# Full expert blocks by table and one last block per expert, a preparing step ahead of the blocks, and gathers taken one by one between the feature operations

## The chip, the cores and the metric

One core of a Trainium2 chip runs the whole program. The metric is the device time of one execution in microseconds (us), median of several runs. TensorE, VectorE, ScalarE, GpSimd and SyncE (here only an issuer of DMAs) each run their own stream of instructions and meet at semaphores. In the rows PE is TensorE's matmul, PEld its weight load, DVE VectorE, ACT ScalarE, POOL GpSimd, SPq the sequencer of SyncE.

## The reference

Input x has 32 batches of 256 tokens of 128 elements. With xn = layernorm(x) the result is x + attention(xn) + ffn(xn):

```python
# attention: 16 heads of 8, per batch, over 256 tokens
cov = einsum('bhsd,bhtd->bhst', q - mean(q), k - mean(k)) / 8
scores = cov + var(q)[..., :, None] * var(k)[..., None, :] / 8
out = softmax(scores) @ v @ Wo
# ffn: causal attention across the 32 batches for each token place, then experts
x1 = x + causal_attention(layernorm(x))
hn2 = layernorm(x1)
topw, topi = top_k(softmax(hn2 @ router_w.T), 2)        # 2 of 8 experts
y = sum over the two: gate * (gelu(hn2 @ w1[e]) @ w2[e])  # 128 -> 256 -> 128
return x1 + y
```

## The kernel before

The program has three stages, and every engine's stream is written out in their order.

**Groups** (`group_step`, g = -3 to 16, 16 groups of 16 token places by 32 batches = 512 rows each): the causal attention, x1, the router. The two chosen experts' rows of a token, `rows`, are scattered by GpSimd's indirect DMAs into the HBM tensor `token_rows` at places `spots`; each expert has a region of its own there. `scatter(n, p, k)` issues four of them, for k = 0 and 1. `add_x` adds x to x1 into `acc`, which SyncE stores as `out_base`. Step 16 is the last of the stage, with only the router part of group 15; GpSimd's step 15 ends with `add_x(15)`, then `scatter(14, .., 1)`, `scale_x(1)` and `scatter(15, .., 0)`.

**Blocks** (`blocks`, 40 blocks of 512 rows): VectorE's `block_table` counts each expert's rows and makes a table of 40 starts and owners. With C rows an expert has as many blocks as 512 goes into C, rounded up; its last start is clamped so that the block ends with the expert's rows, and so it overlaps the block before it, which is why the stores keep an order. SyncE loads rows and weights six blocks ahead (`load_block`), TensorE transposes the rows (`turn`), multiplies up (`expert_up`), ScalarE takes the gelu (`hidden`), TensorE multiplies down (`expert_down`), VectorE multiplies by the gate (`expert_y`, three buffers `y_sb`), and GpSimd stores to `expert_out` (`store_blocks`, line 620), each store after the one before has landed:

```python
pool.wait_ge(s_y, i + 1)
if i >= 1:
    pool.wait_ge(s_yd[(i - 1) % YBUFS], 16 * ((i - 1) // YBUFS + 1))
```

**Steps** (`step(b, p)`, b = -1 to 32, one batch each; `rest_steps`): the attention of xn. A step goes through 16 heads. TensorE makes the column scores of batch b's heads and, four heads ahead, the row scores of batch b + 1 (from head 12 on of b + 2), of which VectorE takes maxima (`take_max`, `rowmin`, line 1182); the maxima become `shift` rows (`split_shift`, lines 1190 and 1192, at heads 3 and 12). ScalarE takes the exponentials. Batch b + 3 is prepared at the same time: VectorE's statistics at head 0, GpSimd's `scale_x` (lines 488, 490, tile `centre`), ScalarE's `normalise_x` at head 5, TensorE's transposes at head 7 and projection at head 9, ScalarE's `features`, then GpSimd's `features_stack`: four operations of squares (lines 500 to 508), the high part (510, 513), the low part (two copies, 516, and two subtracts, 518). TensorE transposes that stack (`stack_transposes`, line 721) in the next step, half 0 at head 9 and, one step on, half 1 at head 0 (`PE_AT`), and VectorE copies it out. GpSimd also gathers the expert rows of batch b by four indirect DMAs (`gather`, line 604, tile `ysel`, which the rows call `xg`) and sums them (`add_selected`, line 610); TensorE adds the sum at head 13 of the next step (`project_out`). `own.next()` is GpSimd's wait for its own last operation.

Each engine has the order: groups, blocks, then steps -1 to 32. Step -1 has no scores of its own: it makes the maxima of batch 0 and the first four of batch 1, and prepares batch 2. TensorE starts the blocks after four maxima, and begins step -1 when y of the last block is done.

## Time and profile before

| | |
|---|---|
| median of 3 runs | 1063.92 us (1061.32 to 1064.46) |
| profiled execution, own time | 1062.73 us |
| its span, first to last instruction | 1060.8 us |
| busy, share of the span | PE 85%, DVE 77%, ACT 66%, POOL 58% |
| mean granted TensorE clock | 0.937 of full speed |
| groups, blocks, steps | to about 366 us; 382 to 540; 540 to the end |

The profile is of one execution. Starts are counted from the first instruction. A busy share says how long instructions of an engine were under way, and matmuls overlap, so a full TensorE need not be at its peak; what sets the time is read from waits, stage by stage.

### The profile page before, as it was taken

The page shows a single profiled execution, that of the slowest core. Times are in us where ns is not written, and L with a number is a line of the kernel's source. Part 1 is how long each engine was busy: PE and PEld are TensorE (multiplying, and loading weights), DVE is VectorE, ACT ScalarE, POOL GpSimd, SP SyncE. Part 2 cuts the span into 40 slices and gives each one's busy share as a digit, 9 for nine tenths or more (in the row PEclk, how much of TensorE's full clock was granted, in tenths as well). Part 3 has the DMA queues.
Part 4 walks back from the last instruction along what each step waited for, and adds up shares of the span by engine and source line. Part 5 has one row for each costly group of instructions (what it writes and reads, how often), then busy time and mean ns, then how long its engine had stood idle before and what let it go on. Part 6 is the DMA issues. An engine that isn't in the chain of part 4 may idle for free.

```text
span 1060.8 us, 34080 instructions
## 1 busy us (share of the span) xinstructions
PE 901.2 (85%) x11947; PEld 563.1 (53%) x11962; DVE 819.3 (77%) x2175; ACT 696.2 (66%) x1395; POOL 613.1 (58%) x886
## 2 busy tenths in 40 slices
PE   3677887878886449999969999999999999999997
PEld 2445554655654237877734555555555555555543
DVE  4876877788787435555558999999999999999980
ACT  3666877788784213433316778777777877777774
POOL 4145666667677531211127777777777777777741
PEclk9688999899999659999977999999999999999998
DMA  5419322223221147777521111111111111111111
GB/s 154 80 31 200 74 53 56 60 53 72 52 50 35 43 132 214 215 219 204 172 61 38 38 48 51 40 42 46 48 34 46 51 33 48 46 46 36 43 42 31
DMA packets 110825, 80.52 MB, mean 76 GB/s; under 512 B 23297, under 2 KB 97921, under 8 KB 110721
## 3 DMA queue, kind: packets, MB, share of 16 engines
q1 hardware_dynamic: 99328, 51.78, 19.5%
q0 software_dynamic: 11392, 27.35, 8.8%
q8 instruction: 66, 1.08, 0.5%
q14 instruction: 39, 0.31, 0.1%
HBM read 44.83 MB, written 33.73 MB: 74 GB/s over the span
## 4 chain that ended last, share of the span: by engine, by line
PE 41%; DVE 18%; issue 16%; DMA 12%; ACT 10%; POOL 2%; DVEq 1%; POOLq 0%; SPq 0%; ACTq 0%
PE bank L682 34%; DMA expert_out<-y 11%; DVE rowmin L1182 7%; PE bank L721 3%; ACT Vexp L1657 2%; DVE QKT L1173 2%; ACT gxb L1685 2%; PE bank L804 1%; ACT rows L1700 1%; DVE smax L1227 1%; ACT hnT L1628 1%; PE bank L783 1%; POOL token_rows L554 1%; DVE sprobT L1238 1%; ACT prob L1664 1%
## 5 line engine op out<-in xcount | busy, mean ns | idle before, releaser
L1613 ACT ACTIVATE prob<-bank 128x512 f32<-128x512 f32 x512 | 293.1, 603 | 88.7 <-PE bank L682 86.2
L1182 DVE TENSOR_REDUCE rowmin<-bank 128x2 f32<-128x512 f32 x512 | 325.6, 683 | 32.0 <-PE bank L682 29.6
L682 PE MATMUL bank<-QKT 32*128 32x256 f16 x2048 | 184.7, 276 | 28.4 <-DVE rowmin L1182 21.9
L604 POOL DMA_INDIRECT xg<-expert_out,place x128 | 125.1, 978 | 46.7 <-issue 31.0
L554 POOL DMA_INDIRECT token_rows<-rows,spots x128 | 127.2, 994 | 40.2 <-issue 32.3
L682 PEld LDWEIGHTS bank<-QKT 32*128 32x128 f16 x2048 | 67.0, 93 | 143.4 <-DVE rowmin L1182 68.7
L682 PE MATMUL bank<-prob,V 128*25 128x256 f32 x2048 | 137.8, 387 | 0.5 <-ACT prob L1613 0.5
L1772 ACT ACTIVATE hmid<-bank,wrow,up_scale 128x512 f32<-128x512 f32 x80 | 58.0, 773 | 107.7 <-PE bank L682 107.7
L620 POOL DMA_DIRECT2D expert_out<-y x40 | 30.2, 755 | 134.9 <-DMA expert_out<-y 106.5
L682 PEld LDWEIGHTS bank<-prob,V 128*25 128x25 f32 x2048 | 50.5, 103 | 52.0 <-issue 26.6
L682 PE MATMUL bank<-wrow,hmid 128*128 128x128 f32 x640 | 77.8, 275 | 0.0
L682 PEld LDWEIGHTS bank<-wrow,hmid 128*128 128x128 f32 x640 | 74.6, 192 | 0.1
L1491 DVE TENSOR_TENSOR y<-bank,xrow 128x512 f32<-128x512 f32 x40 | 27.7, 692 | 54.3 <-DMA expert_out<-y 50.6
L1227 DVE TENSOR_REDUCE smax<-bank 128x16 f32<-128x512 f32 x64 | 43.8, 684 | 32.4 <-PE bank L682 29.8
L500 POOL TENSOR_TENSOR sq<-feat 128x512 f32<-128x512 f32 x32 | 33.3, 1040 | 59.0 <-ACT feat L1584 58.9
L682 PE MATMUL bank<-turned,wrow 128*128 128x512 f16 x240 | 61.0, 392 | 7.4 <-DVE turned L1483 7.2
L682 PE MATMUL bank<-hnT,in_wT 128*128 128x512 f32 x64 | 42.6, 752 | 25.0 <-ACT hnT L1628 21.5
L539 POOL TENSOR_TENSOR rstd<-var,minus_half 128x4 f32<-128x4 f32 x16 | 16.6, 1037 | 64.4 <-DVE minus L1274 64.4
L682 PE MATMUL bank<-Kexp,gqT 32*32 32x128 f32 x2048 | 39.6, 308 | 16.5 <-issue 16.4
L1238 DVE STREAM_TRANSPOSE sprobT<-prob 128x512 f32<-128x512 f32 x64 | 43.4, 697 | 9.0 <-ACT prob L1664 8.6
L1481 DVE CAST turned<-bank 128x512 f16<-128x512 f32 x40 | 27.5, 686 | 27.4 <-PE bank L989 27.4
L1644 ACT ACTIVATE Kexp<-bank,head_bias,quad_mask 128x512 f32<-128x512 f32 x64 | 44.4, 775 | 5.5 <-PE bank L682 5.5
(229 smaller groups left out, 1945.9 us busy)
## 6 DMA issues: line engine op xcount, KB each, us to landing
xrow<-token_rows SPq DMA_DIRECT2D x40, 258.0 KB, 3.0
wrow<-weight_rows SPq DMA_DIRECT2D x40, 257.0 KB, 3.2
expert_out<-y POOLq DMA_DIRECT2D x40, 256.0 KB, 2.8
token_rows<-xrow SPq DMA_DIRECT2D x16, 258.0 KB
xg<-in_L_attn_x SPq DMA_DIRECT2D x64, 64.0 KB, 2.2
x_in<-in_L_attn_x SPq DMA_DIRECT2D x32, 128.0 KB
out_base<-acc SPq DMA_DIRECT2D x64, 64.0 KB
base_t<-out_base SPq DMA_DIRECT2D x32, 128.0 KB
```

What stands on the lines that cost most here:

```text
L500: pool.tensor_tensor(sq[:].rearrange(flat), eight, eight, ALU.mult).then_inc(s_pool, 1)
L554: pool.indirect_dma_start(token_rows, bass.IndirectOffsetOnAxis(spots[p][:, j:j + 1], 0), rows[p][:, k, t, :].bitcast(U32), None).then_inc ...
L604: pool.indirect_dma_start(ysel[p][:, k, st, :].bitcast(U32), None, expert_out, bass.IndirectOffsetOnAxis(place[p][:, st, k:k + 1], 0)).the ...
L620: pool.dma_start(expert_out[bass.ds(at, BLK), :].rearrange("(s p) e -> p s e", p=P), y_sb[i % YBUFS][:].bitcast(U32)).then_inc(s_yd[i % YB ...
L682: return pe.matmul(o, l, r, start=start, stop=stop, skip_group_check=True)
L721: ins = pe.transpose(m[:, a, g, st], stack[p][:, a, st, h:h + TILE_ROWS, :].rearrange("p h k -> p (h k)"), identh[:])
L1182: dve.tensor_reduce(rowmin[h // 8][:, :, h % TILE_ROWS, h // TILE_ROWS % HALF], row_scores[i % 3][:].rearrange("p (s t) -> p s t", s=ST), ...
L1227: dve.tensor_reduce(smax[:, r, :], ps, AX.X, ALU.max).then_inc(s_dve, 1)
L1238: dve.transpose(sprobT[:, r].rearrange("p h s -> p (h s)"), sprob[:, r].rearrange("p h s -> p (h s)")).then_inc(s_spT[r], 1)
L1613: act.activation(prob[:, h % 8].rearrange("p t s -> p (t s)"), col_scores[h % 2][:], ACT.Exp, scale=exp_register).then_inc(s_exp, 1)
L1644: ins = act.activation(Kexp[:, :, j, :], head_bank[:].rearrange("p (n t) -> p n t", n=GPOS), ACT.Identity, bias=head_bias[:, j:j + 1], sca ...
L1772: act.activation(hmid[i % 2][c][:], up_bank[c][:], ACT.Gelu, bias=w[:, c:c + 1], scale=up_scale[:, 0:1]).then_inc(s_mid, 1)
```

## The change

1. **Table for the full blocks only.** `FULL` = 32 entries of starts and owners, of blocks filled to the last row (512 goes into C, rounded down). Then every expert has exactly one last block, whose start `tail_at` is max(C - 512, 0) in its region. There are 40 blocks as before. `block_numbers` makes the constant parts ahead of the counts, the running sums are made in three doubling steps instead of seven, and the limits go. The stores of the full blocks wait for no other store; the first last block waits for all full ones, and the last blocks wait for none among them.
2. **Step -1 ahead of the blocks** on GpSimd, TensorE, VectorE and ScalarE, with `shift_out(0, 1)` of step 0 behind it; SyncE keeps it behind its block loads. TensorE's waits ahead of `turn(0)` grow to the end of that step (`s_half[0]` 2, `s_feat` 3, `s_sht[1]` 1, `s_max` 20).
3. **GpSimd's step.** `features_stack` is split in three. `features_low` runs in the next step; `add_selected` does too; the four gathers stand between the pieces. `add_x` of a group moves behind `scatter(g - 1, .., 1)` and `scales(g + 3)`.

GpSimd's order in one step of the steady loop is, before (`DMA` is a gather, `xg` its tile, `sq` and `feat` the features):

```order
L488 TENSOR_TENSOR rstd<-var_x,minus_half 128x2
L490 TENSOR_TENSOR centre<-minus_mean,rstd 128x2
L597 ISA
L600 TENSOR_TENSOR spare<-epsilon 1x1
L604 DMA xg<-expert_out,place 128x128 x4
L500 TENSOR_TENSOR sq<-feat 128x512
L502 TENSOR_TENSOR sq<-sq 128x64x4
L505 TENSOR_TENSOR sq<-sq 128x64x2
L508 TENSOR_TENSOR sq<-sq 128x64
L510 TENSOR_SCALAR feat<-sq,var_scale 128x64
L513 CAST stack<-feat 128x64x9
L516 COPY stack<-stack 128x32x9 x2
```

and now, from the start of a step to its squares:

```order
L489 TENSOR_TENSOR rstd<-var_x,minus_half 128x2
L491 TENSOR_TENSOR centre<-minus_mean,rstd 128x2
L616 ISA
L617 TENSOR_TENSOR xg<-xg 128x256
L604 ISA
L607 TENSOR_TENSOR spare<-epsilon 1x1
L611 DMA xg<-expert_out,place 128x128
L521 COPY stack<-stack 128x32x9 x2
L523 TENSOR_TENSOR stack<-feat,stack 128x32x9 x2
L611 DMA xg<-expert_out,place 128x128
L497 REGISTER_ALU
L501 TENSOR_TENSOR sq<-feat 128x512
```

The sum of the rows (L617) and the low part (L521, L523) are those of the batches before, and stand ahead of the squares of this step; the other two gathers follow the squares and the high part.

TensorE's order ahead of block 0 (`xrow`) was:

```order
L682 MATMUL bank<-wqk,xnT 128x2x128 x2
L682 MATMUL bank<-QKT 128x256 x8
L989 MATMUL bank<-ident,xrow 128x128 x4
L682 MATMUL bank<-turned,wrow 128x512 x6
L989 MATMUL bank<-ident,xrow 128x128 x4
```

and is now, from the transposes of batch 2 in step -1 on:

```order
L724 MATMUL bank<-ident,xn 128x128 x2
L712 MATMUL bank<-QKT 128x256 x4
L751 MATMUL bank<-identh,stack 128x128 x8
L712 MATMUL bank<-wqk,xnT 128x2x128 x2
L712 MATMUL bank<-QKT 128x256 x8
L834 MATMUL bank<-identh,shift 16x128 x2
L712 MATMUL bank<-QKT 128x256 x4
L1019 MATMUL bank<-ident,xrow 128x128 x4
L712 MATMUL bank<-turned,wrow 128x512 x6
```

The row scores (`QKT`), the stack and shift transposes and the projection of step -1 moved from behind the last block to ahead of the first.

The diff, cut (renamed and new small tiles and most of the table are left out):

```diff
@@ -65,7 +65,8 @@
 COLS = TOPK * TILES
 BLK = 512
 SUBS = BLK // P
-BLOCKS = TOPK * NB * NS // BLK + NE
+FULL = TOPK * NB * NS // BLK
+BLOCKS = FULL + NE
 CAP = NB * NS + BLK
 XROWS = NE * (CAP + BLK)
 ROWW = E + 1
...
@@ -489,7 +490,7 @@
                 pool.wait_ge(s_pool, own.next())
                 pool.tensor_tensor(centre[:], minus_mean[:], rstd[:], ALU.mult).then_inc(s_rstd, 1)
 
-            def features_stack(n, p):
+            def features_squares(n):
 
                 pool.wait_ge(s_feat, n + 1)
                 if positive(n - 1):
@@ -507,11 +508,15 @@
                 pool.wait_ge(s_pool, own.next())
                 pool.tensor_tensor(sq[:, :, :, 0], sq[:, :, :, 0], sq[:, :, :, 1], ALU.add).then_inc(s_pool, 1)
                 pool.wait_ge(s_pool, own.next())
...
+
+            def features_high(p):
                 pool.tensor_scalar(feat[:, :, :, D], sq[:, :, :, 0], var_scale[:, 0:1], None,
                                    ALU.mult).then_inc(s_pool, 1)
                 pool.wait_ge(s_pool, own.next())
                 pool.tensor_copy(parts[p][:, :, 0:FEAT], feat[:].rearrange(flat)).then_inc(s_pool, 1)
                 pool.wait_ge(s_pool, own.next())
+
+            def features_low(p):
                 for a in range(2):
                     pool.tensor_copy(slots[p][:, a, :, 1 + a, :], slots[p][:, a, :, 0, :])
...
@@ -575,21 +580,23 @@
                     scale_x(0)
                 if tail:
                     scales2(g)
-                    add_x(g, r)
                 if late:
                     scatter(g - 1, 1 - p, 1)
                 if isinstance(g, int) and g == GROUPS - 2:
-                    features_stack(0, 0)
+                    features_squares(0)
+                    features_high(0)
+                    features_low(0)
                 if isinstance(g, int) and g == GROUPS - 1:
                     scale_x(1)
                 if ahead:
                     scales(g + 3)
                 if tail:
+                    add_x(g, r)
                     scatter(g, p, 0)
                 if isinstance(g, int) and g == -3:
                     clear_values()
...
-            def gather(n, p):
+            def gather_ready(n, p):
 
                 if isinstance(n, int) and n == 0:
                     for k in range(YBUFS):
@@ -599,11 +606,11 @@
                     pool.wait_ge(s_pr_ps, n - 1)
                 pool.tensor_tensor(spare[:], epsilon[0:1, 0:1], epsilon[0:1, 0:1], ALU.add).then_inc(s_pool, 1)
                 pool.wait_ge(s_pool, own.next())
-                for k in range(TOPK):
-                    for st in range(ST):
-                        pool.indirect_dma_start(ysel[p][:, k, st, :].bitcast(U32), None, expert_out,
-                                                bass.IndirectOffsetOnAxis(place[p][:, st, k:k + 1], 0)
-                                                ).then_inc(s_sel[p], 16)
+
+            def gather(p, k, st):
+                pool.indirect_dma_start(ysel[p][:, k, st, :].bitcast(U32), None, expert_out,
+                                        bass.IndirectOffsetOnAxis(place[p][:, st, k:k + 1], 0)
+                                        ).then_inc(s_sel[p], 16)
 
             def add_selected(n, p):
                 pool.wait_ge(s_sel[p], n * 32 + (64 - 32 * p))
...
@@ -613,10 +620,14 @@
 
                 pool.wait_ge(s_table, 1)
                 for i in range(BLOCKS):
-                    at = pool.value_load(table[0:1, 0, i:i + 1], min_val=0, max_val=XROWS - BLK)
+                    if i < FULL:
+                        at = pool.value_load(table[0:1, 0, i:i + 1], min_val=0, max_val=XROWS - BLK)
+                    else:
+                        at = pool.value_load(tail_at[0:1, i - FULL:i - FULL + 1], min_val=0, max_val=XROWS - BLK)
+                    if i == FULL:
+                        for k in range(YBUFS):
+                            pool.wait_ge(s_yd[k], 16 * ((FULL - k + YBUFS - 1) // YBUFS))
                     pool.wait_ge(s_y, i + 1)
-                    if i >= 1:
-                        pool.wait_ge(s_yd[(i - 1) % YBUFS], 16 * ((i - 1) // YBUFS + 1))
                     pool.dma_start(expert_out[bass.ds(at, BLK), :].rearrange("(s p) e -> p s e", p=P),
                                    y_sb[i % YBUFS][:].bitcast(U32)).then_inc(s_yd[i % YBUFS], 16)
 
@@ -624,14 +635,30 @@
                 prev, cur, nxt, prep, norm = present(b)
                 own.count = 0
                 pool.sem_clear(s_pool)
+                first = isinstance(b, int) and b == 0
                 if norm:
                     scale_x(b + 3)
+                if prev:
+                    add_selected(b - 1, 1 - p)
+                if cur and not first:
+                    gather_ready(b, p)
+                    gather(p, 0, 0)
+                if prep and not first:
+                    features_low(p)
+                if cur and not first:
+                    gather(p, 0, 1)
+                if norm:
+                    features_squares(b + 3)
+                if first:
+                    gather_ready(b, p)
+                    gather(p, 0, 0)
+                    gather(p, 0, 1)
                 if cur:
-                    gather(b, p)
+                    gather(p, 1, 0)
                 if norm:
-                    features_stack(b + 3, 1 - p)
+                    features_high(1 - p)
                 if cur:
-                    add_selected(b, p)
+                    gather(p, 1, 1)
 
             def masks():
                 pool.memset(onesb[:], 1.0)
...
@@ -670,7 +697,10 @@
                     pool.wait_ge(s_vones, q + 1)
 
             run_groups(pool, group_step)
-            features_stack(1, 1)
+            features_squares(1)
+            features_high(1)
+            step(-1, 1)
+            features_low(0)
             store_blocks()
             rest_steps(pool, step)
...
@@ -1016,9 +1046,10 @@
 
                 pe.wait_ge(s_spot, GROUPS)
                 pe.wait_ge(s_zeroed, 2)
-                pe.wait_ge(s_half[0], 1)
-                pe.wait_ge(s_feat, 2)
-                pe.wait_ge(s_max, 4)
+                pe.wait_ge(s_half[0], 2)
+                pe.wait_ge(s_feat, 3)
+                pe.wait_ge(s_sht[1], 1)
+                pe.wait_ge(s_max, H + LEAD)
                 turn(0)
                 for i in range(BLOCKS):
                     expert_up(i)
@@ -1101,6 +1132,7 @@
                             pv(b, p, g)
 
             run_groups(pe, group_step)
+            step(-1, 1)
             blocks()
             rest_steps(pe, step)
 
@@ -1352,6 +1384,8 @@
                         bias_columns()
                     for r in range(1, QUAD):
                         block_transposes(g, r)
+                if isinstance(g, int) and g == GROUPS:
+                    block_numbers()
                 if late:
                     choose_values(g - 1)
                     choose_experts(g - 1)
...
-            def block_table():
...
+            def block_numbers():
...
                 dve.memset(number[:, 0:1], 0.0).then_inc(s_dve, 1)
...
-                dve.tensor_scalar(limit_at[:, 0:NE], count[:], -float(BLK), 0.0, ALU.add, ALU.max)
...
+                dve.tensor_scalar(row_end[:], number[:], float(BLK), float(BLK), ALU.mult, ALU.add).then_inc(s_dve, 1)
...
+            def block_table():
...
+                                  row_end[:, 0:most].unsqueeze(1).broadcast_to([1, NE, most]), ALU.is_ge)
+                dve.tensor_scalar(tail_row[:], count[:], -float(BLK), 0.0, ALU.add, ALU.max).then_inc(s_dve, 1)
...
-                for e in range(1, NE):
+                dve.tensor_copy(tail_at[:], tail_row[:])
...
+                for k in range(3):
...
+                    dve.tensor_tensor(ends[k][:, d:NE], last[:, d:NE], last[:, 0:NE - d], ALU.add).then_inc(s_dve, 1)
...
-                    dve.tensor_tensor(ends[:, e:e + 1], ends[:, e - 1:e], filled[:, e:e + 1], ALU.add).then_inc(s_dve, 1)
...
-                dve.tensor_tensor(past[:], number[:].unsqueeze(2).broadcast_to([1, BLOCKS, NE]),
...
-                dve.tensor_tensor(begin[:], begin[:], limit[:], ALU.min).then_inc(s_dve, 1)
...
+                dve.tensor_tensor(past[:], number[:].unsqueeze(2).broadcast_to([1, FULL, NE]),
...
@@ -1548,6 +1580,7 @@
             for i in range(LEAD):
                 take_max(0, i)
             dve.memset(pv_bank[:], 0.0).then_inc(s_zeroed, 1)
+            step(-1, 1)
             blocks()
             rest_steps(dve, step)
 
@@ -1787,7 +1820,7 @@
                         copy_out(b - 1)
                     if h == ACT_AT["features"] and norm:
                         features(b + 3)
-                    if h == ACT_AT["shift1"] and cur:
+                    if h == ACT_AT["shift1"] and cur and not (isinstance(b, int) and b == 0):
                         shift_out(b, 1)
                     if h == ACT_AT["v"] and nxt:
                         v_out(b + 1, 1 - p)
@@ -1803,6 +1836,8 @@
             run_groups(act, group_step)
             act.wait_ge(s_scales, 1)
             act.reg_load(exp_register, exp_scale[0:1, 0:1].bitcast(U32))
+            step(-1, 1)
+            shift_out(0, 1)
             blocks()
             rest_steps(act, step)
 
@@ -1924,11 +1959,16 @@
                 k = i % XBUFS
                 if i >= XBUFS:
                     sp.wait_ge(s_y, i - XBUFS + 1)
-                at = sp.value_load(table[0:1, 0, i:i + 1], min_val=0, max_val=XROWS - BLK)
-                of = sp.value_load(table[0:1, 1, i:i + 1], min_val=0, max_val=(NE - 1) * P)
+                if i < FULL:
+                    at = sp.value_load(table[0:1, 0, i:i + 1], min_val=0, max_val=XROWS - BLK)
+                    of = sp.value_load(table[0:1, 1, i:i + 1], min_val=0, max_val=(NE - 1) * P)
+                    weights = weight_rows[bass.ds(of, P), :]
+                else:
+                    at = sp.value_load(tail_at[0:1, i - FULL:i - FULL + 1], min_val=0, max_val=XROWS - BLK)
+                    weights = weight_rows[(i - FULL) * P:(i - FULL + 1) * P, :]
                 sp.dma_start(xrow[k][:].bitcast(U32), token_rows[bass.ds(at, BLK), :].rearrange("(s p) c -> p s c", p=P)
                              ).then_inc(s_bx[k], 16)
-                sp.dma_start(wrow[k][:].bitcast(U32), weight_rows[bass.ds(of, P), :]).then_inc(s_bx[k], 16)
+                sp.dma_start(wrow[k][:].bitcast(U32), weights).then_inc(s_bx[k], 16)
 
             def clear(at):
 
@@ -1965,7 +2005,7 @@
             for p in range(2):
                 sp.wait_ge(s_accd[p], 64 * GROUPS // 2)
                 sp.wait_ge(s_placed[p], 16 * GROUPS // 2)
-            rest_steps(sp, step)
+            rest_steps(sp, step, -1)
             for p in range(2):
                 sp.wait_ge(s_out[p], 16 * NB // 2)
 
```

## Rows read from the trace of the kernel before

**Rows 1.** The chain that ended last, shares of the span by line.

```profile
PE bank L682 34%; DMA expert_out<-y 11%; DVE rowmin L1182 7%; PE bank L721 3%; ACT Vexp L1657 2%; DVE QKT L1173 2%; ACT gxb L1685 2%; PE bank L804 1%; ACT rows L1700 1%; DVE smax L1227 1%; ACT hnT L1628 1%; PE bank L783 1%; POOL token_rows L554 1%; DVE sprobT L1238 1%; ACT prob L1664 1%
```

**Rows 2.** Windows: us, busy us and (x) instructions by engine, PEclk, DMA share, GB/s.

```profile
395.00:427.00 32.00, 32.00 (x238) 25.73 (x236) 18.86 (x28) 13.01 (x18) 5.41 (x7) 1.00 0.66 193
...
540.00:576.00 36.00, 28.18 (x215) 13.99 (x216) 26.61 (x59) 15.31 (x31) 18.20 (x30) 0.63 0.14 39
656.00:1000.00 344.00, 328.93 (x3906) 180.62 (x3906) 321.98 (x668) 269.74 (x579) 257.72 (x397) 1.00 0.16 44
```

**Rows 3.** Timeline (start us, us, engine, line, operation): VectorE's y; TensorE's last down projection.

```profile
395.15 0.69 DVE L1491 TENSOR_TENSOR y<-bank,xrow 128x512 f32<-128x512 f32 x1 [0.37 <-PE bank L682]
...
426.82 0.69 DVE L1491 TENSOR_TENSOR y<-bank,xrow 128x512 f32<-128x512 f32 x1 [0.37 <-PE bank L682]
...
539.18 0.69 DVE L1491 TENSOR_TENSOR y<-bank,xrow 128x512 f32<-128x512 f32 x1 [2.70 <-DMA expert_out<-y]
...
535.77 0.39 PE L682 MATMUL bank<-wrow,hmid 128*128 128x128 f32 x2
```

**Rows 4.** Timeline of GpSimd in group step 15, and VectorE's last table operations.

```profile
350.60 1.26 POOL L563 TENSOR_TENSOR acc<-x,xg 128x512 f32<-128x512 f32 x1
352.03 1.04 POOL L554 DMA_INDIRECT token_rows<-rows,spots  x1 [0.17 <-issue]
...
372.71 0.17 DVE L1475 CAST table<-owner 1x40 int32<-1x40 f32 x1
```

**Rows 5.** Chain of waits ahead of block 0: start us, us, what.

```profile
374.85 2.27 DMA token_rows<-rows,spots
...
382.31 1.10 PE bank L989 x4
```

**Rows 6.** Timeline of GpSimd, VectorE and TensorE behind the blocks, steps -1 to 1.

```profile
547.38 0.74 POOL L488 TENSOR_TENSOR rstd<-var_x,minus_half 128x2 f32<-128x2 f32 x1
548.20 0.20 POOL L490 TENSOR_TENSOR centre<-minus_mean,rstd 128x2 f32<-128x2 f32 x1
...
556.03 2.47 DVE L1182 TENSOR_REDUCE rowmin<-bank 128x2 f32<-128x512 f32 x4
...
558.00 1.03 PE L721 MATMUL bank<-identh,stack 128*128 128x128 f16 x8
...
575.62 0.62 PE L721 MATMUL bank<-identh,stack 128*128 128x128 f16 x8
```

**Rows 7.** Timeline of GpSimd in a step of the steady loop.

```profile
780.12 1.09 POOL L604 DMA_INDIRECT xg<-expert_out,place  x1 [0.51 <-POOL spare L600]
781.51 0.94 POOL L604 DMA_INDIRECT xg<-expert_out,place  x1 [0.30 <-issue]
...
786.78 1.04 POOL L500 TENSOR_TENSOR sq<-feat 128x512 f32<-128x512 f32 x1 [1.83 <-ACT feat L1584]
...
789.60 0.56 POOL L510 TENSOR_SCALAR feat<-sq,var_scale 128x64 f32<-128x64 f32 x1
...
791.02 0.87 POOL L516 COPY stack<-stack 128x288 f16<-128x288 f16 x2
791.85 1.42 POOL L518 TENSOR_TENSOR stack<-feat,stack 128x288 f16<-128x288 f32 x2
793.22 0.74 POOL L610 TENSOR_TENSOR xg<-xg 128x256 f32<-128x256 f32 x1
...
794.72 0.19 POOL L490 TENSOR_TENSOR centre<-minus_mean,rstd 128x2 f32<-128x2 f32 x1
...
795.59 1.08 POOL L604 DMA_INDIRECT xg<-expert_out,place  x1 [0.51 <-POOL spare L600]
```

**Rows 8.** Timeline of VectorE and TensorE in the same step.

```profile
780.85 0.33 DVE L1190 TENSOR_SCALAR shift<-rowmin 128x16 f16<-128x16 f32 x1
...
787.79 0.18 DVE L1190 TENSOR_SCALAR shift<-rowmin 128x16 f16<-128x16 f32 x1
...
784.53 0.62 PE L721 MATMUL bank<-identh,stack 128*128 128x128 f16 x8
```

85 lines of the change are left out of this document (39 added, 46 removed).

## The prediction

> **What bounds the kernel now.** I read the chain of waits first, then windows by stage, then each engine's timeline at the seams. The chain [rows 1] names matmuls for a third of the span and, second, the stores `expert_out<-y` with 11%: in the expert stage the pacing is done by a DMA. The windows [rows 2] show three regimes: from 395 to 427 us TensorE has no gap and full clock; from 540 to 576, the seam between expert blocks and attention, it is busy 28 of 36 us at a granted clock of 0.63, most of that time on the lower of its two levels (1.2 of 2.4 GHz), after 3 us without work; from 656 to 1000, steady attention, TensorE (329 of 344 us) and VectorE (322) are both almost full and GpSimd has a quarter free.
>
> *Expert stage.* y(0) starts at 395.15 and y(9) at 426.82 [rows 3]: 3.52 us a block, and VectorE waits only 0.37 us for TensorE there. From y(9) to y(39) at 539.18 it is 112.36 us for 30 blocks, 3.75 us each, because each store waits for the one before it. TensorE had done its last down projection at 536.16 (535.77 + 0.39) and y(39) came 3 us later.
>
> *Ahead of the blocks.* The last scatter is issued at 374.85 and lands 2.27 us later; TensorE transposes block 0 at 382.31 [rows 5]. In between the only large work is GpSimd's for batch 1.
>
> *Behind the blocks.* Step -1 needs `centre` of batch 2, which GpSimd makes only after its last store, at 548.40; the last row maximum ends at 558.50; the stack transposes of step 0 (its first head) are at 558.00 and those of step 1 at 575.62, 17.62 us later [rows 6], against 15.47 us in the steady loop (two first gathers, 780.12 and 795.59 [rows 7]). I take 15.5.
>
> **The change, part by part** (the sum is against the profiled execution: span 1060.8, own time 1062.73; the median of the runs, 1063.92, is 1.2 higher).
>
> 1. `add_x` behind the scatter. In steps 0 to 14 the same GpSimd work is only permuted inside one step, and `gb`, which comes 1.3 us earlier, feeds ScalarE work that then waits longer for TensorE: nothing. In step 15 the add (1.26 us) stood ahead of the scatters, and everything up to block 0 hangs on them: they start 0.17 us after `rbias` instead of at 352.03 [rows 4], 1.2 us earlier.
>
> 2. Table. It becomes shorter, but was ready at 372.9 with the scatters landing at 377.1 [rows 4, 5]: nothing now. The maxima behind it start some 3 us sooner and step -1 with them, which the next term needs.
>
> 3. Step -1 ahead of the blocks. TensorE now waits for 20 maxima, so block 0 waits for the whole step. GpSimd sets it: its last scatter is issued from 374.85 on, takes 0.94 (the length of a second gather [rows 7]) and now ends at 374.6; squares and high part of batch 1 take 4.2 (786.78 to 790.95 for the same operations [rows 7]): 378.8; `scale_x(2)` takes 1.0 [rows 6]: 379.85. From `centre` to the last maximum it was 558.50 - 548.40 = 10.1 [rows 6], at the same low clock: block 0 starts at 390.0, 7.7 us later than at 382.31. The low part of batch 1 (2.25, the time of the two copies and two subtracts [rows 7]) ends at 382.1, as TensorE gets there.
>
> 4. Stores without order. y(0) comes 12.84 us after block 0's transposes [rows 3, 5]: 402.8. At 3.52 a block y(38) starts at 536.6. The last block has no transposes and no up projection behind it: y(39) starts about 1.9 later, 538.5, and ends at 539.2, where before it ended at 539.87. So the blocks end 0.7 us earlier although they began 7.7 later. The one wait left, all full stores ahead of the first of the last eight, stands on GpSimd beside a 3.5 us block and costs nothing.
>
> 5. Step 0 right behind the blocks. The stack transposes came 0.6 after y(39) in step -1; now it is step 0 that begins so: 539.8 for 558.00, 18.2 us less. TensorE arrives warm, so step 0 takes 15.5 for 17.6: another 2.1. Together 20.3 us.
>
> 6. GpSimd's new order, the term that takes back. The low part of the features moves into the next step, behind `scale_x`, the sum of the gathered rows and the first gather, and TensorE needs it at head 9. That closes a loop: squares, low part, stack transposes, projection, features, squares. Each piece, from [rows 7]: four square operations 2.7 (786.78 to 0.1 before 789.60); gather 0.51 + 1.09; high part 1.37; gather 1.6 (7.3 so far); `scale_x` 1.0 (8.3); the sum waits for the gather issued at 6.2. The nearest row for its landing is the scatter's 2.27 with an issue of 0.94 [rows 5]; with 1.09 of issue I take 2.4: 8.6. Sum of the rows 0.74, spare 0.2, gather 1.6: 11.1. Low part 2.27: 13.4. From the transposes at 784.53 [rows 8] to the next squares at 786.78: 2.25. The loop is 15.7 us, 0.2 more than the step. Before, the low part was ready at 793.27 and used a step later at head 9, 6.8 us of slack; now there is none. The first round is longer: in step 0 the spare operation and three gathers stand between squares and high part, two of them at 0.30 + 0.94: loop 18.4, 2.9 over the step. So 2.9 + 28 x 0.18 = 7.9 us are lost, TensorE waiting at head 9. Bounds for the loop: 15.4 if a landing takes no longer than `scale_x` and the semaphore gaps are 0.30 as between two gathers, 16.2 if the gather, which reads rows of HBM instead of writing them, lands 0.5 us later. I take 15.7, nearest the rows.
>
> The Trainium skill, in "DMA: Bandwidth & Descriptors", section "Rules for kernel authors", says to issue a DMA early, compute, and wait for it late. That speaks against this edit, which leaves `scale_x` alone between the last gather and its wait, and puts whatever landing remains into the loop. With that page's fixed cost of about 2.0 us for a transfer, as an estimate, the sum would wait about nothing and the loop be some 15.4 us.
>
> Sum: -20.3 + 7.9 = -12.4; 1062.7 becomes 1050.3, and with the 1.2 us between profiled run and median **1051.5**.
>
> **The rivals.**
>
> *A. The loop does not bind.* GpSimd keeps 15.5 or less and only the first round costs 2 us. Moreover the pair `shift` at head 3 now meets a gather in progress (0.33 us, ending with it at 781.2 [rows 7, 8]; the one at 787.79 takes 0.18) and would meet GpSimd between two operations: 0.15 x 29 = 4 us. Time 1063.9 - 20.3 + 2 - 4 = 1041.6 at the best, 1045.6 without that. For it: GpSimd has a quarter free. Against it: the loop's pieces add up past the step. The Trainium skill, in "SBUF — State Buffer", section "Who interferes with whom", has VectorE's two-port modes and GpSimd exclude each other for a whole instruction; by that rule such a gain exists, and the trace agrees with the 0.33. Chance 0.25.
>
> *B. The loop is longer than 16.1.* Slower than before needs (20.3 - 2.9) / 28 = 0.62 us a step over 15.5, that is a landing 0.45 us later than I take, or VectorE holding GpSimd up at each gather. At 16.3: 28 x 0.8 = 22.4, and 1063.9 - 20.3 + 2.9 + 22.4 = 1069. No row shows a gather's landing, which speaks neither way; GpSimd's operations have the same durations in every step shown, which speaks against. Loops of 15.9 to 16.1 (1058 to 1063.5) have 0.08, slower ones 0.09.
>
> *C. The stores gain nothing:* unordered stores run into the loads, and the pace stays 3.75 a block instead of 3.52. For it: the chain has 11% on these stores [rows 1], and the DMA engines are at 0.66 [rows 2]. Against: that share is the one of the stretch that ran at 3.52. It costs 30 x 0.23 = 7: 1058.5. Chance 0.1. That the change doesn't store a row twice or skip one is clear from its table, so "does nothing" has no share of its own.
>
> **How the numbers follow.** Forecast (loop 15.5 to 15.9, pace 3.52): 0.48, 1046 to 1058, likeliest 1051.5. A 0.25, B's two parts 0.17, C 0.1. The range for 8 in 10 reaches from A at its best, 1041, to a loop of 16.05, 1062. A measurement of this kernel tells 0.3%, 3.2 us, from no change: faster is the forecast, A, C and most of the loops below 16.0, 0.84; within 0.3% (1060.7 to 1067.1) 0.09; slower 0.07.
>
> **What would show it.** Right: y(0) near 403 and 3.52 us a block to y(38); stack transposes of step 0 within 1 us of y(39); clock 1.0 through step 0; GpSimd's feature subtract ending just ahead of the transposes at head 9, with TensorE waiting there for it each step; gathers' first to first 15.7. Wrong: block 0 before 388 or after 393; GpSimd waiting over 1 us for `feat` in the steady loop (then A); the row sum over 1 us behind `centre` (then B); VectorE's y waiting for stores (then C).

## The result: 1034.84 us, faster, and below the forecast range

The changed kernel took 1034.84 us (median of 4 runs, 1033.28 to 1042.30), the kernel before 1064.19 on the same chip: a ratio of 0.9731, interval 0.9680 to 0.9783. Forecast were 1051.5 and 1041 to 1062. The direction was right; the gain was 17 us larger than forecast. Some runs of a kernel are over 1.5% above its fastest; the ratios here and below leave those out, and for the first chip of the experiments, where six of the seven runs of the kernel before were such (1267.58 to 1273.43, the seventh 1248.46), no ratio is given. The profile below is of the 1042.30 run, the slowest of the four.

The chain that ended last, by line; against [rows 1] the stores are gone from it and GpSimd's feature and gather work has come in.

```profile
PE bank L712 36%; POOL xg L611 4%; POOL stack L523 3%; DVE rowmin L1214 3%; PE bank L751 2%; POOL stack L521 2%; PE bank L1019 2%; POOL rstd L489 2%; POOL sq L501 2%; ACT Vexp L1690 2%; ACT gxb L1718 2%; ACT rows L1733 1%; DVE sprobT L1270 1%; POOL sq L503 1%; POOL token_rows L559 1%
```

The windows of [rows 2], of the kernel after (columns as there: busy us and instructions of TensorE, its weight loads, VectorE, ScalarE, GpSimd, then granted clock, DMA share, GB/s). The seam (540 to 576) is warmer than before, 0.76 for 0.63, and holds 288 matmul records for 215; the steady stretch does 3998 in the time in which it did 3906.

```profile
395.00:427.00 32.00, 30.39 (x193) 22.78 (x194) 15.25 (x23) 11.80 (x16) 4.68 (x6) 0.85 0.43 132
540.00:576.00 36.00, 30.25 (x288) 15.36 (x288) 25.12 (x55) 20.54 (x43) 18.28 (x27) 0.76 0.12 35
656.00:1000.00 344.00, 334.41 (x3998) 183.84 (x3995) 314.88 (x679) 268.65 (x590) 268.65 (x407) 1.00 0.17 45
```

Timeline around the blocks, answering [rows 3, 5, 6]: block 0's transposes, y of block 0, of block 9 and of the last, then the stack transposes of steps 0 and 1.

```profile
392.50 1.09 PE L1019 MATMUL bank<-ident,xrow 128*128 128x128 f32 x4 [1.60 <-DVE rowmin L1214]
...
406.03 0.69 DVE L1523 TENSOR_TENSOR y<-bank,xrow 128x512 f32<-128x512 f32 x1 [0.78 <-PE bank L712]
437.70 0.69 DVE L1523 TENSOR_TENSOR y<-bank,xrow 128x512 f32<-128x512 f32 x1 [0.37 <-PE bank L712]
541.08 0.69 DVE L1523 TENSOR_TENSOR y<-bank,xrow 128x512 f32<-128x512 f32 x1 [1.10 <-PE bank L712]
...
542.15 0.62 PE L751 MATMUL bank<-identh,stack 128*128 128x128 f16 x8
559.17 0.62 PE L751 MATMUL bank<-identh,stack 128*128 128x128 f16 x8
```

Nine blocks take 31.67 us, 3.52 each, and that pace holds to block 37: no y waits for a store any more. From y(0) to y(39) it is 135.05 us, before 144.03. Step 0 follows at once, but takes 17.0 us. Then GpSimd's first square operation of step 1, of step 2 and of the last full step, with the wait of TensorE in step 1:

```profile
570.56 1.01 PE L751 MATMUL bank<-identh,stack 128*128 128x128 f16 x8 [2.48 <-POOL stack L523]
...
574.09 1.04 POOL L501 TENSOR_TENSOR sq<-feat 128x512 f32<-128x512 f32 x1 [2.52 <-ACT feat L1617]
...
589.77 1.04 POOL L501 TENSOR_TENSOR sq<-feat 128x512 f32<-128x512 f32 x1 [1.74 <-ACT feat L1617]
...
983.83 1.04 POOL L501 TENSOR_TENSOR sq<-feat 128x512 f32<-128x512 f32 x1 [1.23 <-ACT feat L1617]
```

From 589.77 to 983.83 are 26 steps of 15.16 us (15.13 without the last three); the kernel before has 15.50. This is the surprise: 0.37 us a step gained, where I had 0.2 lost.

Where it comes from shows in the groups of VectorE's two last statistics operations (line, operation, tiles, count | busy us, mean ns), from 656 to 1000 us: of the kernel before,

```profile
L1165 DVE TENSOR_SCALAR var_x<-mv 128x2 f32<-128x2 f32 x22 | 10.5, 476 | 0.8
L1166 DVE TENSOR_SCALAR minus_mean<-mv 128x2 f32<-128x2 f32 x22 | 9.3, 422 | 0.0
```

and after:

```profile
L1197 DVE TENSOR_SCALAR var_x<-mv 128x2 f32<-128x2 f32 x22 | 3.8, 172 | 0.8
L1198 DVE TENSOR_SCALAR minus_mean<-mv 128x2 f32<-128x2 f32 x22 | 3.6, 162 | 0.0
```

In the old order they stand beside GpSimd's second part of the features. Timeline of the kernel before, steady loop:

```profile
776.38 1.43 POOL L518 TENSOR_TENSOR stack<-feat,stack 128x288 f16<-128x288 f32 x2
...
777.09 0.74 DVE L1166 TENSOR_SCALAR minus_mean<-mv 128x2 f32<-128x2 f32 x1
777.74 0.68 DVE L1182 TENSOR_REDUCE rowmin<-bank 128x2 f32<-128x512 f32 x1
```

An operation on 128 x 2 numbers ends (777.83) with the pair of subtractions (777.81, within the 0.02 us of rounding), and the row minimum behind it, which TensorE needs, starts 0.57 us late. One of the two, in turn, is hit in every step. Hit, such an operation takes 0.74 us, otherwise 0.15 to 0.17. In the changed kernel that place of GpSimd holds a gather and the statistics are not prolonged.

One meeting is left, in both kernels. At head 12 the second `shift` operation stands beside GpSimd's second square operation in every step; its group has a mean of 420 ns (before 429) although it takes 0.17 to 0.18 us alone. Timeline of the kernel after:

```profile
757.33 0.73 POOL L503 TENSOR_TENSOR sq<-sq 128x256 f32<-128x256 f32 x1
757.35 0.74 DVE L1224 SCALAR_TENSOR_TENSOR shift<-rowmin,shift 128x16 f16<-128x16 f32 x1
```

It ends at 758.09, the square operation at 758.06. No run moved it, so what it costs is open.

The loop that I had called the binding one exists, too: squares, low part, stack transposes, projection, features, squares. Timeline of GpSimd and TensorE after, one round:

```profile
761.86 1.01 POOL L611 DMA_INDIRECT xg<-expert_out,place  x1 [0.28 <-POOL stack L516]
762.89 0.74 POOL L489 TENSOR_TENSOR rstd<-var_x,minus_half 128x2 f32<-128x2 f32 x1
...
764.48 0.72 POOL L617 TENSOR_TENSOR xg<-xg 128x256 f32<-128x256 f32 x1 [0.57 <-DMA xg<-expert_out,place]
...
765.66 1.05 POOL L611 DMA_INDIRECT xg<-expert_out,place  x1 [0.28 <-POOL spare L607]
766.73 0.86 POOL L521 COPY stack<-stack 128x288 f16<-128x288 f16 x2
767.55 1.41 POOL L523 TENSOR_TENSOR stack<-feat,stack 128x288 f16<-128x288 f32 x2
769.11 0.61 PE L751 MATMUL bank<-identh,stack 128*128 128x128 f16 x8 [0.23 <-POOL stack L523]
```

GpSimd waits there for nothing but the landing (0.57 us), and TensorE 0.23 us for GpSimd, as it does in about half of the steps (0.17 to 0.42 us).

### The profile page after: what moved, and what is told of

The parts are those of the page before. It is cut to its first block, busy times and chain, and to the rows that moved or that the text cites. A ratio compares the mean times of both kernels' runs of the same rounds, so it can differ in the third digit from the quotient of the medians.

```text
span 1040.6 us, 34011 instructions
## 1 busy us (share of the span) xinstructions
PE 902.4 (87%) x11962; PEld 564.5 (54%) x11962; DVE 805.8 (77%) x2168; ACT 688.4 (66%) x1395; POOL 619.2 (59%) x886
## 3 DMA queue, kind: packets, MB, share of 16 engines
q1 hardware_dynamic: 99328, 51.78, 20.3%
## 4 chain that ended last, share of the span: by engine, by line
PE 43%; POOL 19%; issue 14%; DVE 13%; ACT 10%; POOLq 0%; DVEq 0%; DMA 0%; ACTq 0%
PE bank L712 36%; POOL xg L611 4%; POOL stack L523 3%; DVE rowmin L1214 3%; PE bank L751 2%; POOL stack L521 2%; PE bank L1019 2%; POOL rstd L489 2%; POOL sq L501 2%; ACT Vexp L1690 2%; ACT gxb L1718 2%; ACT rows L1733 1%; DVE sprobT L1270 1%; POOL sq L503 1%; POOL token_rows L559 1%
## 5 line engine op out<-in xcount | busy, mean ns | idle before, releaser
L1646 ACT ACTIVATE prob<-bank 128x512 f32<-128x512 f32 x512 | 290.1, 602 | 81.0 <-PE bank L712 80.6
L611 POOL DMA_INDIRECT xg<-expert_out,place x128 | 128.0, 1000 | 33.0 <-POOL spare L607 9.4
L501 POOL TENSOR_TENSOR sq<-feat 128x512 f32<-128x512 f32 x32 | 33.3, 1041 | 50.4 <-ACT feat L1617 50.4
L712 PE MATMUL bank<-causal,onesb 128*128 128x512 bf16 x180 | 48.4, 395 | 0.0
```

The lines of the kernel that those rows point to most:

```text
L501: pool.tensor_tensor(sq[:].rearrange(flat), eight, eight, ALU.mult).then_inc(s_pool, 1)
L611: pool.indirect_dma_start(ysel[p][:, k, st, :].bitcast(U32), None, expert_out, bass.IndirectOffsetOnAxis(place[p][:, st, k:k + 1], 0)).the ...
L712: return pe.matmul(o, l, r, start=start, stop=stop, skip_group_check=True)
L1646: act.activation(prob[:, h % 8].rearrange("p t s -> p (t s)"), col_scores[h % 2][:], ACT.Exp, scale=exp_register).then_inc(s_exp, 1)
```

## Experiments

Theory P: the step became shorter because VectorE's statistics no longer meet a subtraction of GpSimd. Rivals: O, the gain comes from other parts of the change; L, the loop of term 6 is what sets the pitch. "Pitch" is the time between first squares of successive steps. All medians are beside the kernel before on the same chip. The edits are cut to what tells them apart.

The chips were of two kinds. On two, the kernel before took 1271 and 1278 us; on the others 1061 to 1065, as in the runs that the prediction was made from. Kernels that were first measured on one of the two slower chips were measured again on another; where only the slower kind was had, the text says so.

**GpSimd's order alone** (the kernel before, with the changed kernel's order of a step; step 0 has the gathers behind the squares as there):

```diff
-gather(b, p)
-features_stack(b + 3, 1 - p)
-add_selected(b, p)
+add_selected(b - 1, 1 - p); gather_ready(b, p); gather(p, 0, 0); features_low(p)
+gather(p, 0, 1); features_squares(b + 3); gather(p, 1, 0); features_high(1 - p); gather(p, 1, 1)
```

> The kernel before with only GpSimd's new step order (low part in the next step, four gathers between the pieces). Theory P (VectorE's small operations no longer wait for a GpSimd operation in progress, so the step itself falls): 28 steps of 15.13 for 15.50 are 10.4 us less, the longer first round gives 4 to 6 back: 1058 to 1060. Theory L (the blind prediction's loop of 15.7): 8 us more than before, 1072. Theory O (the shorter step comes from the other parts, the stores or step -1): step stays 15.5, total 1064 to 1068.

> The kernel before with GpSimd's new order of a step alone, a second time, since the chip of the first four runs gave 1271 us for the kernel before and its traces of the old order show TensorE standing 1 to 2.7 us in most steps ahead of head 8, which neither trace of the first pair shows. If the steady gain belongs to GpSimd's order (squares pitch 15.50 to 15.13), this gives about 1064 - 26 x 0.37 + 3 for the long first round = 1057 us where the kernel before takes 1064, with a pitch of 15.1 to 15.2. If the gain needs step -1 ahead of the blocks (another phase of the engines), the pitch stays at 15.5 and the time is 1064 to 1067.

First chip: 1145.09 us (1138.63 to 1151.88) for 1270.97 (1248.46 to 1273.43), pitch 15.2. Second: 1059.38 (1055.47 to 1070.59) for 1065.32, ratio 0.9976 (0.9934 to 1.0018), which can't be told from no change; pitch 15.14. The steady gain belongs to the order alone: in a kernel that still does step -1 behind the blocks the pitch is that of the changed one. The first two rounds take back 5.8 us of it: they last 17.83 and 18.99 us for 17.06 and 13.99.

**All but that order** (the changed kernel with the old order of a step):

```diff
-add_selected(b - 1, 1 - p); gather_ready(b, p); gather(p, 0, 0); features_low(p); ...
+gather_ready(b, p); 4 x gather; features_squares(b + 3); features_high(1 - p); features_low(1 - p)
+add_selected(b, p)
```

> The changed kernel with GpSimd's step in the old order. Theory P: the step is 15.50 again, 10.4 us more, and step 1 is no longer held up at head 9, 4 to 6 us less: 1039 to 1042 against the changed kernel's 1035. Theory O: the step stays 15.13 and the total is 1030.

> The changed kernel with GpSimd's old order of a step. If the order gave the steady gain, squares pitch 15.5 and 1035 + 10 - 3 = 1040 to 1046 us. If the gain came from the step that was moved ahead or from the stores, the pitch is 15.1 and the time 1031 to 1035, below the changed kernel by its long first round. If this chip is like the first one, the pitch is 18 to 20 and the time near 1240.

First chip 1241.45 (1237.18 to 1251.27) for 1270.97, ranges that overlap. Second: 1041.83 (1038.13 to 1046.59) for 1065.32, ratio 0.9813 (0.9761 to 0.9865), pitch 15.50. So everything but the order is worth 0.0187 x 1065 = 20 us (14 to 25 by the interval), and O is out for the pitch.

**Stores, table and last blocks alone** (before; step -1 and GpSimd's order as before):

```diff
-if i >= 1:
-    pool.wait_ge(s_yd[(i - 1) % YBUFS], ...)
+if i == FULL:
+    for k in range(YBUFS): pool.wait_ge(s_yd[k], ...)
```

> The kernel before with only the table, the last blocks and the stores without order. Blocks at 3.52 us from y(0) on and y(39) 1.8 us behind y(38): 8 us less than before, 1056. If the stores run into the loads: under 2 us less. The step stays at 15.50 under theory P, falls to 15.13 under theory O (then 1046).

> The kernel before with the new table, the last block of each expert and the stores without order, a second time on another chip. By the prediction's steps the blocks keep 3.52 us to the end instead of 3.75 from the tenth on: 30 x 0.23 = 7 us less, y(39) at 531 to 532 us instead of 539.2, and 1057 to 1058 us where the kernel before takes 1065, ratio 0.993; step -1 still stands behind the blocks. If GpSimd's last stores, or the loads of rows, take the gain back, 1062 to 1066.

Both fell on chips of the slower kind: 1256.07 (1235.04 to 1267.67) for 1270.97, ranges that overlap, and 1269.16 (1255.62 to 1284.03) for 1278.37, ratio 0.9934 (0.9891 to 0.9976), some 8 us. The blocks keep 3.52 us: y(0) to y(39) takes 135.05 us. On the other kind of chip this part was not run by itself, but every trace with the new stores has those 135.0 us there too, and the two with the old ones have 143.5 and 143.8, the kernel before 144.0.

**Statistics at head 1** (the kernel before, one number):

```diff
-DVE_AT = dict(half1=1, out=5, half0=10, statistics=0,
+DVE_AT = dict(half1=1, out=5, half0=10, statistics=1,
```

> The kernel before with VectorE's statistics one head later (0 to 1), which puts them behind the end of GpSimd's second subtract. If the 0.57 us that the last statistics operation waits there is what makes the step 15.5: 15.0 to 15.15, and 1052 to 1054. If that wait was hidden, as the prediction had it: 15.5 and 1064. If only the shift at head 3 counted: 15.5 too.

> The kernel before with VectorE's statistics taken at head 1 instead of head 0, where the last of them stood 0.57 us for GpSimd's subtraction. If that meeting was the 0.37 us a step, the pitch falls to 15.1 to 15.2 and the time to 1053 to 1056 us. If the meeting only moves with the statistics, or if it was hidden, 15.5 and 1062 to 1066; 15.7 or more if at head 1 the statistics stand in the way of a row minimum that TensorE waits for.

First chip: 1294.56 (1289.43 to 1307.69) for 1270.97, slower, at a pitch of 19 to 21: there something else holds the step up (last section). Second: 1053.23 (1050.93 to 1060.41) for 1065.32, ratio 0.9907 (0.9875 to 0.9940), pitch 15.20 (15.08 and 15.32 in turn): 10 us by the ratio, 12 by the medians, and 27 x 0.30 = 8 by the pitch. The same groups, from 656 to 1000 us, of this kernel:

```profile
L1165 DVE TENSOR_SCALAR var_x<-mv 128x2 f32<-128x2 f32 x22 | 3.7, 169 | 0.8
L1166 DVE TENSOR_SCALAR minus_mean<-mv 128x2 f32<-128x2 f32 x22 | 3.6, 162 | 0.0
```

No instruction of GpSimd was touched, and 0.30 of the 0.37 us are there: P holds. The other small meetings hardly change (the pair of `shift` operations 199 and 422 ns, before 233 and 429).

**Both: the changed kernel with the old order and statistics at head 1.**

> The changed kernel with GpSimd's old order of a step, and VectorE's statistics at head 1 instead of 0. In the kernel before, that move alone took the squares pitch from 15.50 to 15.20 and the time from 1065 to 1053 us. If the two are the same gain got in two ways, this gives 1041.8 - 29 x 0.3 = 1033 us, a ratio near 0.970, pitch 15.2, level with the changed kernel. If GpSimd's new order gives something of its own, it stays above 1036.

> The changed kernel with GpSimd's old order of a step and VectorE's statistics at head 1, again, since the first time it ran on a chip that gives 1278 us for the kernel before. Where the kernel before takes 1065: if the statistics' wait is the whole of what GpSimd's order gave, 1033 us and a pitch of 15.2, level with the changed kernel; if the new order gives something of its own, above 1036. On a chip of the other kind: 1270 to 1280, and standstills of ScalarE and VectorE that end 2.1 to 2.2 us after the start of the fourth gather in every step.

On the slower kind 1279.25 for 1278.37, ratio 0.9990 (0.9955 to 1.0025); on the other 1036.27 (1032.88 to 1036.70) for 1061.28, ratio 0.9746 (0.9721 to 0.9772), pitch 15.20. On the latter the one number brings the old order from 0.9813 to 0.9746, 7 us, within the interval of the changed kernel (0.9731). What the new order has beyond it is 15.20 against 15.13, 2 us, less than the intervals can tell.

**Whole first step** (changed kernel; in step 0 GpSimd issues all gathers first and completes the features of batch 3):

```diff
+if first:
+    gather_ready(b, p); 4 x gather
 features_squares(b + 3)
-if first:
-    gather_ready(b, p); gather(p, 0, 0); gather(p, 0, 1)
-gather(p, 1, 0)
+if not first: gather(p, 1, 0)
 features_high(1 - p)
-gather(p, 1, 1)
+if first: features_low(1 - p)
+else: gather(p, 1, 1)
```

> The changed kernel, in whose step 0 GpSimd issues the four gathers while it waits for the features (it sat idle for 10.43 us there) and then makes the whole stack of batch 3, so that step 1 starts without the rest of it. If the loop of squares, second part, transposes, projection and features made the first round 19.45 us, that round falls to 16.5 to 17.2 and the time by 2 to 3 us, ratio to the changed kernel 0.997 to 0.998. If the first round is long because TensorE's clock is low there, it stays at 19 and the time too.

1034.34 (1030.44 to 1035.51) for 1065.32, ratio 0.9715 (0.9666 to 0.9765). The first round falls from 19.45 to 14.70 us in the profiled runs, although the granted clock falls to 0.50 in this step 0 as well, so the loop made most of it long, and not the clock; the median gains 1 to 2 us by the ratios, less than the intervals.

**The loop shortened** (the kernel with the whole first step, and the second part of the features ahead of the step's first gather):

```diff
+features_low(p)
 gather_ready(b, p)
 gather(p, 0, 0)
-features_low(p)
```

> The whole-first-step kernel with the second part of the features ahead of the first gather of each step (2.3 us of work between squares and transposes moved up by the 1.3 us of a gather). If GpSimd's loop is what sets the pitch of 15.1, TensorE's waits for the second part (0.23 to 0.43 us in half of the steps) vanish and the pitch falls to 14.9 to 15.0, 3 to 6 us in all. If TensorE and VectorE set it, the waits vanish, others grow and the pitch stays at 15.1. If a subtraction of GpSimd now meets VectorE's pair at head 3 (0.18 to 0.7 us), the pitch rises to 15.3 to 15.5.

> The second part of the features ahead of the first gather, again. GpSimd's loop through the features falls from 15.0 to 13.8 us by the rows of the changed kernel. Where the kernel before takes 1065: if that loop set 15.13, pitch 14.9 to 15.0 and 3 to 6 us less than 1034; if TensorE and VectorE set it, 15.1 and the same time within 1 us; if a subtraction now meets VectorE's pair at head 3, 15.3 or more.

Slower kind: 1154.43 for 1278.37, ratio 0.9010 (0.8967 to 0.9054). Other: 1031.86 (1028.57 to 1038.35) for 1061.28, ratio 0.9726 (0.9696 to 0.9756). TensorE's waits for the stack are gone from the list of waits and the pitch is 15.22, not less. This run does not judge L, though, because the edit made a new meeting of the kind that P is about: GpSimd's subtractions now stand beside the `shift` pair of head 3. From 656 to 1000 us:

```profile
L1227 DVE SCALAR_TENSOR_TENSOR shift<-rowmin,shift 128x16 f16<-128x16 f32 x45 | 21.7, 481 | 1.6
L1225 DVE TENSOR_SCALAR shift<-rowmin 128x16 f16<-128x16 f32 x45 | 13.7, 305 | 1.6
```

The whole first step alone has 420 and 193 ns, so with two pairs a step VectorE loses 0.35 us a step here. A shorter loop may have gained what this cost. What speaks against L as the sole cause are the two kernels with the old order and the statistics at head 1: they have no such loop (in the old order the low part lies ready 6.8 us before TensorE takes it), TensorE never waits there for the stack, and their pitch is 15.20. So at 15.1 to 15.2 the loop and TensorE with VectorE are about level; what a shorter loop without the new meeting would bring is not shown.

**The loop lengthened** (the kernel with the whole first step, and all four gathers in one burst ahead of the second part):

```diff
 gather_ready(b, p)
-gather(p, 0, 0)
+4 x gather
 features_low(p)
-gather(p, 0, 1) ... gather(p, 1, 0) ... gather(p, 1, 1)
```

> The whole-first-step kernel with all four gathers of a step in one burst ahead of the second part of the features. By the rows of the changed kernel the loop is then squares 2.7, high part 1.4, scale_x 1.0, row sum 0.7, spare 0.2, four gathers 5.1, second part 2.3, to the next squares 2.25: 15.7 us. Where the kernel before takes 1065: if the loop through the features is what sets the pitch, 15.7 and 1034 + 28 x 0.55 = 1049 us, TensorE waiting for the second part each step. If the loop is not felt, 15.1 to 15.2 and 1034 to 1037. On a chip of the other kind: if it is the burst of gathers behind each other that makes ScalarE and VectorE stand still, the pitch is 18 to 21 again and the time near 1250; if it was the old order's place of the gathers, 15.7 to 16.

1149.03 (1146.38 to 1154.13) for 1061.28, ratio 1.0835 (1.0801 to 1.0870): 100 us over my 1049. GpSimd, then TensorE, in its steady loop:

```profile
779.67 0.73 POOL L489 TENSOR_TENSOR rstd<-var_x,minus_half 128x2 f32<-128x2 f32 x1 [3.11 <-DVE minus_mean L1197]
...
788.89 1.03 PE L750 MATMUL bank<-identh,stack 128*128 128x128 f16 x8 [2.62 <-POOL stack L523]
```

Its window from 656 to 976 us (columns as above):

```profile
656.00:976.00 320.00, 276.42 (x2902) 150.02 (x2898) 230.93 (x495) 194.40 (x426) 190.73 (x295) 0.87 0.13 34
```

TensorE waits 2.6 us a step, not 0.6, and the steps last 18 to 21 us at a granted clock of 0.87. My sum of pieces left one edge out: `scale_x` waits for the statistics of the new step (here 3.11 us), so the path that counts begins at head 0 and must reach head 9; from the end of the statistics (3.11 us of wait ahead of 779.67) to TensorE's transposes at 788.89 it is 9.2 us. A wait of TensorE delays the next statistics, and behind the wait the granted clock is lower: 1.00 from 785 to 787 us, 0.50 from 788.9 to 790. An estimate: 15.1 + 2.6 = 17.7 is about the shortest step of this kernel (17.61), so the rest, up to 21, would be the clock's; no run separates the two.

**Idle products around the blocks** (the kernel with the whole first step, plus products of constants on TensorE that nothing reads):

```diff
+def warm(times): times x mm(bank[4], onesb, causal)
 step -1, head 7: + warm(5); heads 8 to 15: + warm(1)
 turn(0)
+warm(3)
 expert_down(BLOCKS - 1)
+warm(3)
```

> The whole-first-step kernel with products of two constants on TensorE that nothing reads: 5 while it waits 4 us in step -1, one per head behind that, 3 ahead of block 0's first products and 3 behind the last down projection. If the low granted clock is what makes the first three blocks take 5.1 us instead of 3.52, and step 0 longer, y(0) comes 3 to 4 us earlier and the time falls by 3 to 5 us, ratio to before near 0.967. If the cold products themselves hold step -1 up, y(0) comes at the same time or later, and the time is the same within 1 us.

> The whole-first-step kernel with idle products on TensorE around the expert stage, again. Where the kernel before takes 1065: if the low granted clock costs the first blocks 1.5 us each, 3 to 5 us less than 1034; if the products hold step -1 up, the same within 1 us.

Slower kind: 1124.73 (1121.04 to 1128.82) for 1278.37, ratio 0.8789 (0.8754 to 0.8825), the lowest there, where the whole first step was not run without the products. Other: 1032.71 (1027.49 to 1034.62) for 1061.28, ratio 0.9715 (0.9687 to 0.9743), the same as without them. y(0) came at 403.63, not earlier than without (402.07), and 11.0 us behind block 0's transposes in both. But the products did not lift the clock: from 392 to 396 us it is 0.50 with and without them, and in step 0 it falls to 0.50 (545 to 550 us) although TensorE no longer waits at the last y. So the run says nothing on what the low clock costs.

Three versions stand at 0.9715 to 0.9726, none told apart from the changed kernel; all are 2.7 to 2.9% below the kernel before.

## Why the prediction was short

- **Terms 1 to 3** (`add_x`, table, step -1 ahead of the blocks) put block 0's transposes at 390.0 and y(0) at 402.8. Measured y(0): 406.03 in the shown profile, and 398.06, 398.97, 402.07, 403.35, 403.63 and 404.25 in the six others with step -1 ahead of the blocks on this kind of chip; block 0 at 392.50, and 385.23 to 392.81 in those. Right on the average; two of the seven (385.23 and 387.84) lie ahead of the bound of 388, and why profiled runs differ by 8 us here is not shown.
- **Term 4** (stores): 3.52 us a block to block 37, the last 1.8 behind its neighbour for 1.9 forecast, end of y(39) 541.8 in the shown run and 533.8 to 540.0 in the six others, for 539.2; the stretch of blocks is 9.0 us shorter. Right. Rival C falls.
- **Term 5** (step 0 right behind the blocks, 20.3 us): the seam closed, 542.15 for 558.00. "TensorE arrives warm" failed: it arrives at a clock of 1.00, but 0.79 us without work at the last y are followed, 3 us later, by 0.50, and step 0 takes 17.0 us for 15.5. In six of the same seven traces the clock falls so (step 0 takes 16.4 to 17.6 us); only the old order's profiled run, with the same 0.79 us, stayed at 1.00 (13.6 us), while the old order with statistics at head 1 did not, so the order does not decide it. Everything but the order was worth 20 us by the ratio (14 to 25) where I had -20.3: the sum fits although its parts differ, and that is in part luck.
- **Term 6** (GpSimd's order, +7.9 us) is the step that failed, in size and in sign. Measured by the ratios: 0.9731 - 0.9813, that is -9 us, by the medians -6, and by the traces -5 (26 x -0.37, and the first rounds some 5 longer than in the old order); the intervals are too wide to choose between these, but all have the other sign than +7.9. Two faults. First, "before it was 15.50" was taken for the floor that the loop is held against; it contained 0.56 us a step of VectorE standing in its own statistics, of which 0.37 reach the pitch, and of these statistics the prediction said nothing. Second, the loop was 15.7 by the rows of the old order and is 15.13 at most: the waits ahead of a gather are 0.27 to 0.28 us where I took 0.51, while the landing that I set at 2.4 is 2.62 (761.86 to 764.48). The lower bound of 15.4 was itself too high. The long first round was right in kind: 19.45 us, 18.4 forecast, 4.7 us of it saved by the whole first step. Between +7.9 and -5 to -9 lie 13 to 17 of the 17 us by which the forecast missed.
- **Rival A** (0.25, 1041.6 at best) had the mechanism, VectorE held up by GpSimd, but at the pair at head 3. There the changed kernel saves little: over the steady stretch the first `shift` operation goes from 233 to 189 ns and the second from 429 to 420. The sign named for A, GpSimd waiting over 1 us for `feat`, did come (1.23 us), but it tells nothing: by the prediction's own pieces (13.4, a gather of some 1.2 behind it, squares at 15.7) it would have come with the loop binding, too. The Trainium skill, "SBUF — State Buffer", section "Who interferes with whom", says that VectorE's two-port modes and GpSimd exclude each other for a whole instruction; the trace agrees, since the 0.74 us end with the pair of subtractions, and the experiment with statistics at head 1 gives 10 us by the ratio. The rule had to be tried on every small VectorE operation, not on one.
- **Rival B** needed a loop 0.6 us over the step. The burst kernel is such a case and costs 88 us more than the kernel before, not 5: my price of 28 times the excess is far too low once TensorE waits.
- The Trainium skill, "DMA: Bandwidth & Descriptors", section "Rules for kernel authors", has a DMA issued early and waited for late. With that page's fixed cost of about 2.0 us, as an estimate, the sum would have waited for nothing. Measured are 2.62 us from issue to landing and a wait of 0.57 us, and the kernel became faster in spite of it.

## What to carry over

A measured step is no floor: before an added chain is held against it, look in each engine's groups for one operation whose mean is far above that of its like (476 ns for 172; 420 ns for 170 still stands in the changed kernel), and ask whether the edit moves what it meets. When a chain ends near the step, price both sides: within the slack it costs nothing, beyond it a wait of TensorE comes back through the next step and the clock. A change whose parts have opposite signs is judged by doing one part alone, twice if the chip differs.

## What the runs showed of the hardware, unexpected

The chips differed far more than the versions. With the old order the kernels take 1241 to 1295 us on two chips and 1036 to 1065 on the others; with the gathers spread over the step, 1125 to 1154 for 1032 to 1059. The pitch tells one part of it: with the old order 18 to 21 us for 15.2 to 15.5, with the gathers one by one 15.2 on both. The other part lies ahead of the blocks: y(0) comes 71 to 77 us later there in each version that ran on both kinds (the changed kernel with the old order 475.39 for 404.25). The old order's cost on those chips is what makes GpSimd's order alone worth 8 to 10% there (1145.09 for 1248.46 to 1273.43) and 0.2% here. On the slower kind a step looks like this (changed kernel, old order, statistics at head 1):

```profile
903.08 0.39 PE L701 MATMUL bank<-QKT 32*128 32x256 f16 x4
903.93 0.94 POOL L611 DMA_INDIRECT xg<-expert_out,place  x1 [0.30 <-issue]
906.08 0.60 ACT L1635 ACTIVATE prob<-bank 128x512 f32<-128x512 f32 x1 [3.97 <-remote]
906.12 1.29 DVE L1203 TENSOR_REDUCE rowmin<-bank 128x2 f32<-128x512 f32 x2 [3.01 <-remote]
```

and its windows there:

```profile
902.00:903.00 1.00, 1.00 (x15) 0.53 (x8) 1.00 (x2) 0.12 (x1) 0.69 (x2) 1.00 0.43 133
903.00:904.00 1.00, 0.47 (x6) 0.11 (x4) 0.11 (x1) 0.00 (x0) 0.69 (x2) 1.00 0.29 70
904.00:905.00 1.00, 0.00 (x0) 0.00 (x0) 0.00 (x0) 0.00 (x0) 0.87 (x1) 1.00 0.29 70
905.00:906.00 1.00, 0.00 (x0) 0.00 (x0) 0.00 (x0) 0.00 (x0) 0.00 (x0) 0.63 0.28 66
906.00:907.00 1.00, 0.19 (x3) 0.14 (x4) 0.88 (x2) 0.92 (x3) 0.00 (x0) 0.50 0.00 0
```

TensorE, VectorE and ScalarE all stand still while the last gathers move 66 to 70 GB/s, and start again when that traffic ends, 1.9 to 2.3 us after the start of the fourth gather in the 30 such steps of this trace from 640 us on. The profile doesn't show what they wait for ("remote"), and no run separates it. On those chips it happens in most steps with four gathers 0.30 us apart, for 1.1 to 1.8 us in some steps with two together, and where the gathers are taken one at a time only in the first and last steps, in which they follow each other after all. On the other kind of chip no trace has such a wait. The burst kernel, which would have tested it, was measured on the other kind only, so the cause stays open.
